# Keys of the routed attention layer: stored once per part, their rows multiplied by the loads in three transfers per half

## What is computed

```python
def expert_step(acc, params):
    qw, qb_, kw, kb_, vw, vb_, ow, ob_, g = params
    q = (x @ qw.T + qb_).reshape(B, S, H, Dh).transpose(0, 2, 1, 3)
    k = (x @ kw.T + kb_).reshape(B, S, H, Dh).transpose(0, 2, 1, 3)
    v = (x @ vw.T + vb_).reshape(B, S, H, Dh).transpose(0, 2, 1, 3)
    scores = jnp.einsum('bhqd,bhkd->bhqk', q, k) * scale
    p = jax.nn.softmax(scores, axis=-1)
    o = jnp.einsum('bhqk,bhkd->bhqd', p, v)
    o = o.transpose(0, 2, 1, 3).reshape(B, S, E) @ ow.T + ob_
    return (acc + o * g[..., None], None)
```

## Time and profile before

| | us |
|---|---|
| median of 3 runs (3921.69 to 3930.07) | 3928.61 |
| the profiled execution | 3943.5 |
| its span, first to last instruction | 3941.8 |
| the routed loop's whole tiles, by the output stores at 2435.3 and 3720.0 (33 tiles apart) | 38.93 each |

### The profile page before, as it was taken

How to read it: one execution, slowest core, us unless ns; L and a number is a source line. 1 busy time by engine, 2 the same in 40 slices (tenths; PEclk the granted TensorE clock), 3 DMA queues, 4 the chain that set the end, 5 groups by cost and what they waited for, 6 DMA issues and landing times. The chain is left out here.

```text
span 3941.8 us, 128182 instructions
## 1 busy us (share of the span) xinstructions
PE 3228.2 (82%) x54382; PEld 2106.8 (53%) x54382; DVE 2957.4 (75%) x3661; ACT 2518.8 (64%) x4870; POOL 598.6 (15%) x1574
## 2 busy tenths in 40 slices
PE   2999999489997997465855539999999999999638
PEld 1666666235554674122433426666666666666414
DVE  5999999358883113997353449999999999999653
ACT  1899999347776343332211219999999999999622
POOL 0001000021100000563003011111111111111220
PEclk7999999779998998898957759999999999999858
DMA  4000000300000000440005864555554545554410
GB/s 117 9 7 10 8 9 6 100 17 11 9 7 2 22 21 28 171 146 9 1 13 139 246 181 121 123 124 127 125 128 119 128 121 126 123 132 117 106 33 11
DMA packets 206648, 300.80 MB, mean 76 GB/s; under 512 B 91780, under 2 KB 136010, under 8 KB 205030
## 3 DMA queue, kind: packets, MB, share of 16 engines
q1 hardware_dynamic: 199446, 281.40, 27.6%
q10 hardware_dynamic: 2048, 6.29, 0.8%
q0 software_dynamic: 4592, 5.05, 0.5%
HBM read 223.72 MB, written 60.20 MB: 72 GB/s over the span
## 5 line engine op out<-in xcount | busy, mean ns | idle before, releaser
L862 ACT ACTIVATE channels_qk<-psum 128x512 f32<-128x512 f32 x3842 | 2061.4, 595 | 271.0 <-PE psum L705 186.0
L924 DVE TENSOR_REDUCE l2f_chunk_max<-psum 128x2 f32<-128x1024 f32 x1144 | 1327.6, 1220 | 66.2 <-PE psum L680 53.1
L924 DVE TENSOR_REDUCE chunk_max<-psum 128x2 f32<-128x1024 f32 (+2 forms) x832 | 916.9, 1158 | 110.1 <-PE psum L680 59.4
L680 PE MATMUL psum<-l2f_k_parts,l2f_q_parts 48*128 48x512 bf16 x2288 | 698.2, 388 | 42.4 <-DVE l2f_chunk_max L924 30.3
L705 PE MATMUL psum<-l2f_q_parts,l2f_k_parts 51*128 51x128 bf16 x8968 | 711.9, 218 | 1.9 <-ACT channels_qk L862 1.4
L726 PE MATMUL psum<-channels_qk,l2f_v_and_ones 128*9 128x128 f32 x17920 | 697.7, 274 | 12.3 <-issue 12.3
L680 PE MATMUL psum<-k_parts,q_parts 48*128 48x512 bf16 (+3 forms) x1664 | 424.6, 382 | 101.7 <-DMA q_parts<-q_rows_dram 72.0
L705 PEld LDWEIGHTS psum<-l2f_q_parts,l2f_k_parts 51*128 51x128 bf16 x8968 | 483.5, 94 | 38.1 <-ACT channels_qk L862 27.4
L726 PE MATMUL psum<-channels_qk,v_and_ones 128*9 128x128 f32 x12544 | 493.1, 276 | 0.6 <-ACT channels_qk L862 0.5
L705 PE MATMUL psum<-q_parts,k_parts 51*128 51x128 bf16 x6272 | 433.1, 219 | 30.6 <-DMA q_parts<-minus_max_rows 10.4
L726 PEld LDWEIGHTS psum<-channels_qk,l2f_v_and_ones 128*9 128x9 f32 x17920 | 386.4, 90 | 117.3 <-issue 18.2
(11 more groups left out here) (479 smaller groups left out, 3219.5 us busy)
## 6 DMA issues: line engine op xcount, KB each, us to landing
l2f_k_parts<-l2f_k_parts_dram SPq DMA_DIRECT2D x588, 192.0 KB, 3.7
l2f_v_and_ones<-expert_v_dram SPq DMA_DIRECT2D x144, 288.0 KB, 4.0
l1a_bc_rows<-ssm_rows_dram SPq DMA_DIRECT2D x32, 512.0 KB, 4.6
expert_v_dram<-l2f_v_and_ones SPq DMA_DIRECT2D x8, 1152.0 KB, 4.4
channels_qk<-ssm_rows_dram SPq DMA_DIRECT2D x16, 512.0 KB
expert_q_dram<-heads_out SPq DMA_DIRECT2D x8, 1024.0 KB, 7.5
l2f_q_parts<-l2f_gathered_q_parts SPq DMA_DIRECT2D x444, 16.0 KB
k_parts<-k_rows_dram ACTq DMA_DIRECT2D x32, 192.0 KB, 7.3
```

What stands on the lines that cost most here:

```text
L680: last = nc.tensor.matmul(c.ps[:, 2 * (n % 2) + j, 0:width], at.q[64 * j:64 * j + ROWS, tile % SLOTS, pair, :], kx(tile)[64 * j:64 * j + R ...
L862: nc.scalar.activation(at.prob[:, s % 4, j, 0:kts, :].rearrange("p k q -> p (k q)"), c.ps[:, ring.bank(i, n), 0:kts * 2 * P], ACT.Exp, sca ...
L924: v.tensor_reduce(at.mx[:, 4 * g + 2 * pp:4 * g + 2 * pp + 2, chunk], c.ps[:, 2 * (n % 2):2 * (n % 2) + 2, 0:span.width(tile, chunk)], X, ...
```

## The change

`k_parts_dram` has one row for each channel and part. `store_keys` writes a part with one transfer of 128 rows (both halves together): three for each expert where there were six. `load_keys` loads each part of a half with a transfer of its own, whose source repeats the 8 rows of the part 3, 2 or 1 times: six transfers for each pair of heads where there were two, with the same bytes into SBUF. The row of channel d and number r becomes 8 r + d, for the keys and for the queries (`load_q`). The counts that the engines wait for follow.

```diff
-        self.k_dram = nc.dram_tensor(f"{c.layer}k_parts_dram", [8, 2, NPAIR, HD, NR, T], BF16, kind="Internal").ap()
+        self.k_dram = nc.dram_tensor(f"{c.layer}k_parts_dram", [8, 3, 2, NPAIR, HD, T], BF16, kind="Internal").ap()
...
 def store_keys(at, eng, e, parts, parts_ready, count, parts_stored):
     eng.wait_ge(parts_ready, count)
     for which, part in enumerate(parts):
-        n = len(range(NR)[ROWS_OF_K[which]])
-        for j in range(2):
-            eng.dma_start(at.k_dram[bass.ds(e, 1), j, :, :, ROWS_OF_K[which], :].rearrange("e p d n t -> (e p d) n t"),
-                          part[64 * j:64 * j + 64, :].unsqueeze(1).to_broadcast([64, n, T])).then_inc(parts_stored, 16)
+        eng.dma_start(at.k_dram[bass.ds(e, 1), which].rearrange("e j p d t -> (e j p d) t"), part[:, :]).then_inc(parts_stored, 16)
...
 def load_keys(at, eng, buf, e, pair, k_loaded):
     for j in range(2):
-        eng.dma_start(at.kx[64 * j:64 * j + ROWS, buf, pair, :],
-                      at.k_dram[bass.ds(e, 1), j, pair].rearrange("e d r t -> (e d r) t")).then_inc(k_loaded, 16)
+        for which, rows in enumerate(ROWS_OF_K):
+            n = len(range(NR)[rows])
+            at_row = 64 * j + HD * range(NR)[rows][0]
+            eng.dma_start(at.kx[at_row:at_row + HD * n, buf, pair, :], at.k_dram[bass.ds(e, 1), which, j, pair].rearrange("e d t -> (e d) t")
+                          .unsqueeze(0).to_broadcast([n, HD, T])).then_inc(k_loaded, 16)
...
-    KL = 16 * 2 * 2
+    KL = 16 * 2 * 6
     ML = 16 * 2
-    VL = KL
+    VL = 16 * 4
...
-                            sp.dma_start(at.q[64 * j + r:64 * j + ROWS:NR, slot, :, :],
+                            sp.dma_start(at.q[64 * j + HD * r:64 * j + HD * (r + 1), slot, :, :],
```

More of the change, by code:

```diff
@@ L565, in _ @@
                 for k in range(2):
-                    sp.wait_ge(v_loaded[k], pieces_placed)
+                    sp.wait_ge(v_loaded[k], done * (VL // 2) + VL // 2)
                     for g in range(G):
@@ L2294, in _ @@
                     sp.wait_ge(o_stored[k], 16 * (E // 2 + k))
-                    sp.wait_ge(parts_stored[k], done(96, E // 2))
+                    sp.wait_ge(parts_stored[k], done(48, E // 2))
             @block.gpsimd
@@ L2362, in keys @@
                 def keys(e, k, r):
-                    act.wait_ge(parts_stored[k], done(96, r))
+                    act.wait_ge(parts_stored[k], done(48, r))
                     act.wait_ge(b_loaded[k], r * LOADS + LOADS)
@@ L2380, in _ @@
                 v = nc.vector
-                for n, (s, credit) in enumerate(((parts_ready, 1), (q_psum, 4), (q_ready, 4), (v_ready, 2), (parts_stored[0], 96), (parts_stored[1], 96),
+                for n, (s, credit) in enumerate(((parts_ready, 1), (q_psum, 4), (q_ready, 4), (v_ready, 2), (parts_stored[0], 48), (parts_stored[1], 48),
                                                  (v_stored, 16), (q_stored, 16), (o_stored[1], 16))):
```

## The result

The changed kernel takes 4562.44 us (median of 4 runs, 4558.95 to 4577.97), the kernel before 3929.34 beside it: ratio 1.1622, 95% interval 1.1596 to 1.1649. The forecast was 4728 (4400 to 5450). The profiled execution took 4577.97 us with a span of 4576.3, where before had 3941.8: 634.5 us more.

What follows compares the result with a forecast made beforehand. PE set the loop's pace before; SP's stream, 73% full, would bound it after. Profiled 3943.5 - 45 (stores) + 53 (before the loop) + 791 (loop loads) = 4742.5, median 14.9 below: 4728 us, range 4400 to 5450.

Steps and rivals of the forecast that it cites:

- What bounds: In the routed loop PE sets the pace; SP works 28.4 us of a tile, 73% full, with 10 us free.
- Part 1, the loads: In the routed loop, a half's key issues on SP rise from 0.51 to 2.58 us; 61.5 us a tile, +791 us.
- a small outermost count makes an issue dear: Pricing of key issues on SP: hi and mid at 0.70 us, lo at 0.61, by their outermost counts.
- What is late next: In the loop, once SP falls behind, PE waits for maxima, values and queries; no separate size.
- Part 2, before the loop: 28 halves' keys issued before the first maxima rows: 58 us more, about 5 us of it covered, +53 us.
- Part 3, the stores: Preparation: half the bytes stored, seven experts at 17.5 us instead of 24.0, -45 us.
- the expert's own chain: Preparation's next limit, from ACT's start to DVE's end in one expert: 16.1 us, below the 17.5 forecast.
- Part 4, the queries' rows: Query loads to eight neighbouring partitions instead of every sixth: as many issues and pieces, no change in time.
- One engine: First DMA engine bounds the loop: 61 us a tile (0.197 us a piece) or 86 (0.29); chance 0.20.
- The number of issues alone: In the loop issue shape does not matter: 1.02 us added a half, 44.7 us a tile, 4111 us; chance 0.10.
- The clock: TensorE's clock falls in the loop: PE's tile up to 77.8 us at 1.2 GHz, 5298 us; chance 0.06.
- Hidden loads: SP's free 10 us take a tile's 32 added issues, loop unchanged, preparation's gain left: 3884 us; chance 0.04.

Runs made afterwards that it cites:

- Experiment 4: Kernel before, each half loaded by one transfer whose source is 16 rows, each written to three neighbouring rows, on 16 engines: 3951.13 us, ratio 1.0024.
- experiment 2: Kernel before, a half's 48 rows loaded in three transfers of 24, 16 and 8 plain rows, both sides cut alike: 4201.24 us, ratio 1.0647.
- experiment 6: Changed kernel without 6 of a tile's 12 query transfers: 4430.38 us, ratio 1.1241.
- experiment 3: Kernel before, a half's 48 rows loaded in three transfers of 17, 15 and 16 plain rows: 4713.62 us, ratio 1.1953.
- experiment 1: Changed kernel's stores and layout, but each half loaded by one transfer of 48 neighbouring rows: 3875.59 us, ratio 0.9825.
- experiment 10: Against the kernel before: each part stored once by six stores an expert, halves of two pairs loaded by two transfers in 8 KB pieces: 3957.12 us, ratio 1.0039.
- experiment 9: Changed kernel's stores, but four pairs of a half loaded by two transfers of 24 plain rows by 4 pairs: 3969.31 us, ratio 1.011.

## Why the prediction was right, and where it was off

**What bounds (right).** SP's margin of 10 us a tile was the number on which it turned (the rows from store to store are 19 and not 20; their sum is right). Experiment 4 used some 5 us of it at almost no cost, experiment 2 overran it and paid, and experiment 6 gave back to the tile what it took from SP.

**Part 1, the loads (mechanism right, one term mis-sized, for a wrong reason).** Half after: 0.77 + 0.72 + 0.29 + 3 x 0.19 = 2.35 us, as its start times say (2811.76 to 2814.11), against 2.58 forecast. The registers were right to 0.01 us. Hi and mid at 0.70 came out at 0.76 and 0.69. Lo at 0.61 was the failed term: it costs 0.29. The prices rested on the step "a small outermost count makes an issue dear", read from three rows (L288, L480, L489). Those rows fit another reason as well, and that is the one that experiments 2, 3 and 4 bear out: the queries (8 x 8 rows from 64) and the maxima have sides cut differently, the 48 rows from 48 have not. The two reasons agree on hi and mid and part on lo, where the wrong one was followed; that hi and mid came near is luck, as far as the reason goes. With measured prices SP's sum is 28.4 + 16 x (2.35 - 0.51) = 57.8 us a tile (57.4 with 2.32, the average of all halves), and the stores are 57.73 apart. The loop cost +648.9 (the two loop rows of the table) where +791 was forecast: 142 of the 164.5 us by which the sum was high.

"What is late next" was right in kind. PE waits for values and maxima; the one large wait a tile is for the values, which the forecast named among three. PE is busy 72% and not 62%, since the tile is shorter and, at the lower clock, PE takes longer over it.

**Part 2, before the loop (right).** The +56.2 of the table end at the first of the maxima's rows; the forecast's +53 end behind SP's wait among these rows. That wait was 3.9 us before (the third row at 2347.51) and is gone in the changed kernel (at 2329.01, right behind the second), so to the third row it is +52.3. The nearness is partly luck: 28 halves at the measured 1.84 are 51.5 and not 58, and 4.1 us more went into the query issues, of which the last twelve took 11.58 us for 7.83 (what held them up was not looked into):

```profile
2315.81 11.58 SPq L480 DMA_DIRECT2D l2f_q_parts<-l2f_gathered_q_parts  x12
```

**Part 3, the stores (right in sign, a size off).** -70.8 against -45; experiment 1 alone gives 64 of span. The failed step is the bound "what is late next is the expert's own chain", 16.1 us: the chain was read from ACT's first key activation to the end of DVE's low part, but in the changed kernel the next expert's activation starts before the end of that (2189.37 against 2187.51 + 2.28), so that the period is shorter than the chain. The experts are 15.2 us apart from the third on. The 17.5 itself came from bytes alone, and bytes were not all: halving them in six stores of 64 rows gives 17.7 (experiment 10), in three of 128 rows 15.2, so fewer and larger stores are worth another 2.5 us an expert. In the changed kernel the DMA engines are still 0.95 busy there:

```profile
2085.70:2219.20 133.50, 93.95 (x548) 75.52 (x546) 74.97 (x89) 35.68 (x56) 25.13 (x26) 0.86 0.95 222
```

The first value store of the preparation comes 30 us earlier in the changed kernel (2085.7 against 2115.3), but its first two experts take longer (30.3 and 27.1), and by the third the gain is 21 us. In experiment 1 it starts at 2109.7 and its third is at the same place within 3 us. So this start is no part of the gain that the change can claim; what moves it was not looked into.

**Part 4, the queries' rows (right).** L480 has a median of 609 ns against 607.

**The rivals.** One engine: an estimated load of 53.8 us by the price of experiment 3, and below 55 us by experiment 6, so 3 us or more below SP's. Its chance of 0.20 was not too high. Its slow price of 0.29 was: it would have given 86 us. The number of issues alone: its 44.7 us a tile is what experiment 2 measured (45.7), for a kernel whose sides are cut alike. The clock: 0.83 granted in the loop, between the two levels of 1.2 and 2.4 GHz; PE needs 41.4 us of a tile busy there (286.71 / 400 x 57.73) against 38.3 at full clock, has 16 us free, and loses nothing. Hidden loads: experiment 1 has 16 issues a tile and not 48, so it shows only what would be left if the loads cost nothing, 3875.59, near the 3884 given for it.

## What to carry to other kernels

Before a transfer is split or reshaped, add up the issuing engine's own stream for one period; a queue that is 73% full takes a third more, and what is queued behind the new issues (here the values) is what the computing engines then wait for. Price an issue by whether both sides break into the same steps, and look separately at which engines it reaches: a cheap issue on one engine can be the worst of all. Storing once and multiplying on the way in can pay, if the multiplied rows still come in one transfer on all engines; a layout with overlapping windows is a way to that.

## What the runs showed of the hardware

- An issue of a key load on SP costs 0.32 us if source and target are cut alike (0.24 for 17 rows on one engine, 0.28 for 8 rows on 8), and 0.62 on 16 engines if they are not (0.69 to 0.79 on 2, 3 or 8). Right behind one of the latter on 16 engines the next issue is longer as well: 16 plain rows in experiment 10 took a median of 0.43, the values 0.447 for 0.355.
- A transfer of 17 rows goes to one engine, always the same: 304 pieces a tile took an estimated 0.172 us each, and the whole kernel 20% more time. One of 24 rows goes to 12 (experiment 9's 96 completion packets for 8 transfers).
- With 32 pieces of 4096 bytes into 8 partitions on 8 engines a piece took 0.40 us; with 96 into 24 partitions on 12 engines 0.284; with 16 KB pieces into 24, 16 or 8 partitions on 8 engines 0.276 for each 4096 bytes; with 8 pieces into 8 partitions, a transfer every 0.43 us, 0.229. That it is the bytes at once into few partitions is likely, not shown.
- With keys in pieces of 8 KB the values' pieces on the same engines took 0.200 us, with 4 KB 0.155.
